# Local attention: the residual X added by an identity product on TensorE, the sum copied with its bias by ScalarE

## The reference

```
q, k, v = proj_chunk(Wq, bq), proj_chunk(Wk, bk), proj_chunk(Wv, bv)   # segments of 64, 16 heads of 8
out = _attn(q, k, v)
kd, vd = k[:, :, :, dil_idx, :], v[:, :, :, dil_idx, :]                # every 4th key of a segment
for off in range(1, NN + 1):                                           # NN = 2, w = 1 / 4
    for sign in (-1, 1):
        ...
        cross = _attn(q, kd[:, nc], vd[:, nc])
        out = out + jnp.where(valid[None, :, None, None, None], cross * w, 0.0)
...
return out @ Wo + bo
```

## Time and profile before

| what | value |
|---|---|
| median of 3 runs | 1208.58 us (1206.61 to 1215.52) |
| the profiled execution, its own time | 1208.11 us |
| span of the profiled execution | 1205.7 us, 20228 instructions |
| PE, PEld busy | 1109.7 us (92%), 617.3 us (51%) |
| DVE, ACT, POOL busy | 929.6 us (77%), 811.0 us (67%), 234.6 us (19%) |
| the chain that ended last, by engine | PE 61%, DVE 19%, ACT 12%, issue 6% |
| granted TensorE clock, mean | 0.973 |

### The profile page before, as it was taken

How to read it: one execution, slowest core, us unless ns; L and a number is a source line. 1 busy time by engine, 2 the same in 40 slices (tenths; PEclk the granted TensorE clock), 3 DMA queues, 4 the chain that set the end, 5 groups by cost and what they waited for, 6 DMA issues and landing times.

```text
span 1205.7 us, 20228 instructions
## 1 busy us (share of the span) xinstructions
PE 1109.7 (92%) x7436; PEld 617.3 (51%) x7436; DVE 929.6 (77%) x1521; ACT 811.0 (67%) x1292; POOL 234.6 (19%) x332
## 2 busy tenths in 40 slices
PE   7988899999999989989999899989999888898987
PEld 3333344444444435467766344466666675463354
DVE  4897788777777677767776567699999996577966
ACT  6885655555555664755577735878888876868774
POOL 1000000000000011200000011587878776000000
PEclk9998999999999999989999999989999998998999
DMA  6000111121122100000000000000000000000002
GB/s 177 1 0 1 51 59 65 63 62 61 62 62 62 34 1 1 10 1 2 2 2 1 1 0 1 9 2 2 2 3 2 16 2 2 9 1 1 1 1 70
DMA packets 26361, 27.17 MB, mean 23 GB/s; under 512 B 4171, under 2 KB 17308, under 8 KB 26268
## 3 DMA queue, kind: packets, MB, share of 16 engines
q1 hardware_dynamic: 25936, 25.91, 7.3%
q10 hardware_dynamic: 332, 0.01, 0.0%
HBM read 23.30 MB, written 2.62 MB: 21 GB/s over the span
## 4 chain that ended last, share of the span: by engine, by line
PE 61%; DVE 19%; ACT 12%; issue 6%; POOL 1%; DMA 0%; ACTq 0%; DVEq 0%
PE psum L723 9%; PE psum L734 9%; PE psum L726 4%; PE psum L87 4%; PE psum L983 4%; PE psum L955 3%; DVE arena L2151 2%; PE psum L1634 2%; DVE N L2160 2%; PE psum L1382 2%; DVE arena L2150 2%; ACT ln_std L114 2%; ACT ln_std L116 2%; PE psum L105 1%; PE psum L1965 1%
## 5 line engine op out<-in xcount | busy, mean ns | idle before, releaser
L762 ACT ACTIVATE arena<-psum 128x512 f32<-128x512 f32 x128 | 69.5, 594 | 114.4 <-PE psum L723 114.3
L723 PE MATMUL psum<-arena,weights 128*128 128x512 f32 x256 | 122.3, 600 | 1.7 <-DVE N L128 1.0
L734 PE MATMUL psum<-arena,weights 128*128 128x512 f32 x256 | 120.3, 592 | 0.0
L620 DVE SCALAR_TENSOR_TENSOR arena<-diff,vecs,N 128x512 f32<-128x512 f32 x128 | 95.0, 745 | 0.0
L682 DVE SCALAR_TENSOR_TENSOR arena<-arena,psum 128x512 f32<-128x512 f32 x64 | 43.9, 686 | 62.7 <-PE psum L734 62.6
L2065 ACT ACTIVATE N<-N 128x1024 f32<-128x1024 f32 x64 | 67.8, 1059 | 31.1 <-DVE N L2160 30.4
L1975 PE MATMUL psum<-ident,N 128*128 128x128 f32 x512 | 71.6, 284 | 18.1 <-POOL N L2120 17.7
L723 PEld LDWEIGHTS psum<-arena,weights 128*128 128x128 f32 x256 | 48.5, 192 | 62.5 <-issue 58.1
L734 PEld LDWEIGHTS psum<-arena,weights 128*128 128x128 f32 x256 | 48.6, 190 | 61.2 <-issue 61.2
L1965 PE MATMUL psum<-arena 32*128 32x128 f32 x1024 | 76.1, 288 | 1.6 <-ACT arena L2043 1.4
L1965 PEld LDWEIGHTS psum<-arena 32*128 32x128 f32 x1024 | 63.7, 190 | 25.7 <-issue 11.9
(11 more groups left out here) (330 smaller groups left out, 2505.0 us busy)
## 6 DMA issues: line engine op xcount, KB each, us to landing
arena<-tw_rows SPq DMA_DIRECT2D x64, 256.0 KB, 3.1
out_dram<-arena SPq DMA_DIRECT2D x8, 256.0 KB, 3.6
arena<-in_L_attn_a_x_dram SPq DMA_DIRECT2D x3, 512.0 KB, 6.7
weights<-in_L_attn_a_eWk_dram SPq DMA_DIRECT2D x1, 1024.0 KB, 5.8
arena<-in_L_attn_a_x_dram SPq DMA_DIRECT2D x2, 256.0 KB, 3.9
weights<-in_L_attn_a_eWr_dram SPq DMA_DIRECT2D x1, 512.0 KB, 9.8
tw_rows<-arena SPq DMA_DIRECT2D x2, 128.0 KB, 2.7
tw_rows<-arena SPq DMA_DIRECT2D x1, 256.0 KB, 3.5
```

The source lines that it names most:

```text
L620: op = nc.vector.scalar_tensor_tensor(mixed[:, n % 4, a, :], k.diff[:, q % 2, :], k.vec((f"cm_k{e}", f"cm_r{e}")[a]), before, ALU.mult, AL ...
L723: op = nc.tensor.matmul(k.bank[2 * (n % 2) + h][:], k.eWk[:, e, h * P:(h + 1) * P], mixed[:, n % 4, 0, :], start=True, stop=True)
L734: op = nc.tensor.matmul(k.bank[4 + n % 2][:], k.eWv[:, e, h, :], ks[:, (2 * (n % 2) + h) * CH:(2 * (n % 2) + h + 1) * CH], start=(h == 0), ...
L762: op = nc.scalar.activation(kr[:, h * CH:(h + 1) * CH], k.bank[2 * (n % 2) + h][:], ACT.Relu)
```

## The change

PE's output step first multiplies the chunk of X by the identity into `other` and then accumulates the product with Wo on it. ACT gets a new `keep(t)`, which copies `other` with the bias `bo` to X and raises `sg_x`; it stands in the step of DVE's add, n = 14 + 8t, between ACT's `turned` and `exp`, and the last one behind the loop. DVE's `add` goes.

```diff
         def output(t):
             free()
+            nc.tensor.matmul(other[:], k.ident[:], k.X[:, t * CH:(t + 1) * CH], start=True, stop=False)
             pe.wait_ge(k.sg_ov, t + 1)
-            nc.tensor.matmul(other[:], k.sg_wo, ov[t % 2], start=True, stop=True).then_inc(k.sg_out, 1)
+            nc.tensor.matmul(other[:], k.sg_wo, ov[t % 2], start=False, stop=True).then_inc(k.sg_out, 1)
             last.append((k.sg_x, t + 1))
...
+        def keep(t):
+            act.wait_ge(k.sg_out, t + 1)
+            nc.scalar.activation(k.X[:, t * CH:(t + 1) * CH], other, ACT.Identity, bias=k.vec("bo")).then_inc(k.sg_x, 1)
+
...
             if 0 <= n - 3 < N:
                 turned(n - 3)
+            if n >= 14 and n % 8 == 6:
+                keep((n - 14) // 8)
             if n < N:
                 exp(n)
...
+        keep(TURNS - 1)
...
-        def add(t):
-            at = slice(t * CH, (t + 1) * CH)
-            dve.wait_ge(k.sg_out, t + 1)
-            nc.vector.scalar_tensor_tensor(k.X[:, at], other, k.vec("bo"), k.X[:, at], ALU.add, ALU.add).then_inc(k.sg_x, 1)
-
...
         for n in range(N + 1):
-            if n >= 14 and n % 8 == 6:
-                add((n - 14) // 8)
...
-        add(TURNS - 1)
```

## The result

| kernel | median | runs | lowest to highest |
|---|---|---|---|
| before | 1207.94 us | 8 | 1206.61 to 1215.52 |
| changed | 1219.74 us | 8 | 1215.86 to 1223.47 |

The ratio is 1.0098, with a 95% interval of 1.008 to 1.0116. A second comparison, on a chip on which the kernel before took 1206.61 us, gave 1.0103 (1.0084 to 1.0122).

The account below looks back on a forecast made before the run. DVE was taken to set the pace, PE 0.13 us behind. Seven output products cost 11.05 us, less 0.48 and 0.86 given back (net 9.71), plus 1.41 at the end: 1208.58 + 11.1 = 1219.7 us, range 1211 to 1226.

Parts of the forecast that it names:

- What bounds the stage: In the change's own stage DVE sets the pace, busy 27.73 of 28.00 us, with PE's scores 0.13 us behind.
- turn 5: Output product at PE's step 53, of eight numbered 0 to 7; maxima two steps on were to start 1.35 us later.
- turn 4: Fifth of eight output products, numbered from 0; maxima two steps after its PE step were to start 1.81 us later.
- The identity product at 0.86 us: On PE ahead of each output product: adds 0.86 us, delaying everything behind it there; upper bound 1.06.
- The copy and its place: ACT's 0.67 us copy stands behind the turned-weights copy; PE's value transposes wait 1.18 us for it, delaying DVE's next scores.
- What is given back: Where DVE waited for PE's projections soon after the first four output products: 0.48 and 0.86 us of the loss return.
- The end: After the last output product, the next norm's squares queue behind ACT's last copy: first Ln 1.41 us later.
- Busy time: DVE's busy time over the kernel was to fall by 8 x 0.74 = 5.9 us.
- The first: PE's wait for ACT's copy costs nothing, only the identity product (3.9 us) and stage end (1.4) remain: 1213.9 us; chance 0.17.
- the second: DVE is the only bound and the identity product fits beside it; seven adds free 0.66 us each: 1204.0 us; chance 0.07.
- The third: PE's new wait lowers TensorE's clock after each of seven output products, 11.7 us more: 1231 us; chance 0.08.
- The sum: Over the stage: 9.7 us net behind seven output products plus 1.4 at the stage's end, +11.1 us in all.

## Why the prediction was right, point by point

*What bounds the stage.* Right. VectorE sets the pace and TensorE is 0.13 us behind it in turn 5; the kernel without any add gained what the small leads of the steps allow, 2.1 us, and not 4.6. The one wrong number is turn 4 in the copy-only kernel, early by 0.14 and not 0.06.

*The identity product at 0.86 us.* Right. Output step to scores is 985.50 - 983.59 = 1.91 us, was 1.06: +0.85. Alone it costs 3.9 us in seven turns (predicted 3.9), and doubled 0.86 more in each. The upper bound of 1.06 wasn't needed.

*The copy and its place.* Right, and the larger half. The copy takes 0.68 us (0.67 was taken). TensorE wakes 0.06 us after its end (988.64 + 0.68 = 989.32 to 989.38), as taken, and waits 1.11 us (1.18 was worked out). Each second step is late by 1.02 to 1.04 more. The estimate of 707 ns for the copy by the formula of the Trainium skill ("ScalarE: Activation LUTs", What ACT_TABLE_LOAD costs) is 4% over the measured 682. That keep can't pass the copy ahead of it was shown from the other side: put ahead of it in the list, it started 1.44 us before it and cost nothing.

*What is given back.* Right in place; the size was 0.31 behind turns 0 and 2 and not 0.43. Turn 4, where I had nothing, had another 0.06 ahead of it.

*The end.* Right: +1.53 us for +1.41, shown by the kernel whose last turn is as before. The clock ahead of it, which I had as a bound of 2 us either way and not in the sum, gave 0.7 to 2.3 us back (last section).

*Busy time.* Wrong in size: VectorE's was to fall by 8 x 0.74 = 5.9 us and fell by 4.0. The busy time counts an overlap of two instructions once. The add starts 0.08 us before the end of the instruction ahead of it, so that taking it away frees 0.66 us and not 0.74, as my own sum for the turns had it; and each of the fourteen new waits of VectorE ends such an overlap of 0.08, which adds 0.08. That is 7 x 0.66 - 14 x 0.08 = 3.5 us in the turns, and there the trace has 3.4; the last add makes it 4.2. The variant with the copy ahead, with seven new waits instead of fourteen, has 3.9 less in the turns.

*The rivals.* The first (no cost of the wait) and the second (VectorE alone) are out by the experiments with one part each: ratios 1.0041 for the identity product alone, 1.0042 for the copy alone, 0.9977 for neither. The third is there in one or two of seven turns and not in each, at 1.0 to 1.6 us where it costs; the granted clock of the changed kernel was otherwise 1.00 from 830 to 1005 us. That rival's comparison was too narrow: it set the new wait of 1.1 us against one of 0.68, and the kernel before already had seven of 0.9 to 1.3 us, with no fall behind them in the profile that I had.

*The sum, and some luck in it.* The seven turns and the end were put at 11.1 us; their measured terms are 11.00 - 1.18 + 1.53 = 11.35. Two terms that the sum didn't have nearly cancel, and the clock is the likely cause of both: falls behind a turn add 1.0 us in the mean of the four profiles of the changed kernel, and the stretch from the last maxima to the copy of the last heads is 1.5 shorter in the mean than in the first profile of the kernel before. The two medians differ by 11.8 us. The changed kernel's differs from my number by 0.04 us because I started from 1208.58, the median of three runs, and that of eight is 1207.94. That closeness is luck: single runs of the changed kernel range over 7.6 us, and the stretch ahead of the change was 3.3 us shorter in the profile after and then lost 3.5 in a longer time at the lower clock, neither of which has to do with the edit.

## What to carry to other kernels

Taking work off the busiest engine is worth only the lead that the next one has at that very step; read it as the distance between "input ready" and "start", step by step (here 0.06 to 0.53 us of an add of 0.66), before paying 0.86 us on that next engine. When a read of a shared buffer moves to another engine, what matters is where it stands in that engine's order and who waits for the buffer: the same copy cost 1.03 us in each of seven turns behind a copy that waits for TensorE, and nothing ahead of it.

## What the runs showed of the hardware that I had not expected

- TensorE's clock at the start of the stage. The granted clock is 0.50 at 784 to 788 us in all thirteen profiles. In the nine in which the stage begins early (by 3.3 to 5.2 us against the first profile of the kernel before) it stays low longer, and the steps up to the 14th lose 3.4 to 4.2 us; in the three others nothing.
- The end of the stage: from the last maxima to the copy of the last heads it is 16.45 and 16.19 us in the two profiles of the kernel before, 15.79, 14.19, 15.58 and 14.19 in the four of the changed kernel, and 14.18 or 14.19 in all of the variants with the copy ahead, with the copy on VectorE and without add. In the variants the granted clock was 1.00 there. In the kernel before it fell to the lower level for 7 us, in the changed kernel for some 3.5 us in each of its four profiles. Windows of the first profiles of the kernel before, of the changed kernel and of the variant with the copy ahead, from the last maxima on:

```profile
1009.00:1023.00 14.00, 10.01 (x161) 7.01 (x159) 4.63 (x9) 7.05 (x16) 7.50 (x8) 0.76 0.01 2
1020.00:1034.00 14.00, 10.63 (x177) 7.62 (x175) 4.60 (x8) 6.80 (x15) 7.51 (x8) 0.88 0.01 4
1013.00:1027.00 14.00, 10.50 (x200) 7.00 (x198) 4.51 (x8) 7.33 (x16) 7.51 (x8) 1.00 0.01 2
```

  So 0.7 to 2.3 us for the same instructions are a gain of the changed kernel and of the variants that no step of my sum had. The cause of the clock's choice wasn't tried.
